# Last attention of a two-layer Perceiver kernel: tiles 2 and 3 each go alone from the turn of y to the gate's logits, with the residual added in PSUM

## The reference, cut to what matters

```python
# L1_attn: causal, 16 heads, on the layer-normed x; then a post norm
q, k, v = split(h @ Wqkv.T + bqkv)          # h = layernorm(x)
out = h + softmax(causal(q k^T / 4)) v @ Wout.T + bout
x = x + layer_norm(out) * gamma + beta
# L1_ffn: top-1 mixture of 8 experts on the layer-normed x
logits = layernorm(x) @ Wg + bg
x = x + expert_mlp(argmax(logits))          # 256 -> 1024 -> 256, fp32, GELU
```

## Time and profile before

| | |
|---|---|
| time, median of 3 runs | 528.6 us (528.46 to 528.76) |
| the profiled execution's own time | 528.27 us |
| its span, first to last instruction | 526.4 us |
| PE busy | 501.4 us (95%), 6412 matmul instructions |
| PE weight loads | 355.0 us (67%) |
| DVE busy | 324.5 us (62%) |
| ACT busy | 299.7 us (57%) |
| POOL busy | 124.3 us (24%) |
| DMA | 64.37 MB, mean 122 GB/s |

### The profile page before, as it was taken

The page is one execution under the profiler, slowest core; times in us unless marked ns, Lnnn a source line. Parts: engine busy times, 40 slices in busy tenths (PEclk is TensorE's granted clock), DMA queues, the critical chain, the costliest instruction groups (busy, mean ns, idle before and its releaser), DMA issues.

```text
span 526.4 us, 15176 instructions
## 1 busy us (share of the span) xinstructions
PE 501.4 (95%) x6412; PEld 355.0 (67%) x6426; DVE 324.5 (62%) x672; ACT 299.7 (57%) x512; POOL 124.3 (24%) x218
## 2 busy tenths in 40 slices
PE   7999998899999999789999999999999989999996
PEld 4666676556666665455767767677567658999995
DVE  4652874666666666779899889999358674101101
ACT  2465485866656653477788877887734522233311
POOL 6124126733333333430000000000042033000005
PEclk9999999999999999999999999999999999999999
DMA  8977620135555552900000000000072002998813
GB/s 311 392 269 271 236 78 2 61 76 160 147 159 149 147 158 56 384 11 2 2 4 2 4 2 4 2 4 3 2 259 66 2 0 87 263 367 278 308 60 100
DMA packets 35346, 64.37 MB, mean 122 GB/s; under 512 B 3312, under 2 KB 25328, under 8 KB 34896
## 3 DMA queue, kind: packets, MB, share of 16 engines
q1 hardware_dynamic: 34752, 62.35, 35.9%
q0 software_dynamic: 384, 1.05, 0.6%
q10 hardware_dynamic: 144, 0.01, 0.0%
HBM read 59.40 MB, written 4.00 MB: 120 GB/s over the span
## 4 chain that ended last, share of the span: by engine, by line
PE 81%; DVE 7%; POOL 3%; ACT 3%; issue 2%; DMA 2%; SPq 0%; POOLq 0%; DVEq 0%; ACTq 0%
PE ps L1352 14%; PE ps L1626 10%; PE ps L1758 9%; PE ps L1726 9%; PE ps L1772 7%; PE ps L1640 7%; PE ps L1948 7%; PE ps L1471 2%; PE ps L1484 2%; PE ps L1458 2%; PE ps L1327 2%; PE ps L1435 1%; DVE region L1128 1%; DMA attn_weights<-in_wall 1%; PE ps L1377 1%
## 5 line engine op out<-in xcount | busy, mean ns | idle before, releaser
L1128 DVE TENSOR_REDUCE region<-ps 128x1 f32<-128x512 f32 x192 | 124.2, 687 | 16.2 <-PE ps L1726 16.1
L816 ACT ACTIVATE region<-ps 128x1024 f32<-128x1024 f32 (+1 forms) x112 | 106.0, 963 | 20.9 <-PE ps L1758 20.4
L1726 PE MATMUL ps<-ctx_kT,region 96*32 96x512 bf16 x768 | 82.0, 383 | 1.7 <-DVE region L1128 0.8
L1758 PE MATMUL ps<-region,ctx_kT 98*32 98x512 bf16 x832 | 72.5, 381 | 0.6 <-ACT region L794 0.4
L1772 PE MATMUL ps<-region,ctx_v 128*32 128x128 f32 (+1 forms) x1664 | 70.2, 272 | 0.0
L1626 PE MATMUL ps<-region 128*128 128x512 f16 x264 | 62.9, 379 | 1.0 <-ACT ctx_kT L589 0.7
L1772 PEld LDWEIGHTS ps<-region,ctx_v 128*32 128x32 f32 (+1 forms) x1664 | 56.7, 109 | 9.3 <-issue 0.3
L866 ACT ACTIVATE region<-ps,ctx_v 128x128 f32<-128x128 f32 x88 | 25.2, 368 | 59.7 <-PE ps L1352 59.7
L507 POOL TENSOR_TENSOR region<-region 128x512 f32<-128x512 f32 x33 | 38.2, 1156 | 64.2 <-ACT region L741 62.8
L1640 PE MATMUL ps<-region 128*128 128x256 bf16 x384 | 47.2, 273 | 0.9 <-DVE region L1075 0.9
L1640 PEld LDWEIGHTS ps<-region 128*128 128x128 bf16 x384 | 37.4, 98 | 12.4 <-DVE region L1075 1.7
(11 more groups left out here) (234 smaller groups left out, 821.5 us busy)
## 6 DMA issues: line engine op xcount, KB each, us to landing
region<-in_w SPq DMA_DIRECT2D x15, 1024.0 KB, 8.4
region<-in_ctxT SPq DMA_DIRECT2D x8, 1601.0 KB, 8.5
region<-gates SPq DMA_DIRECT2D x30, 256.0 KB, 3.4
ctx_kT<-in_w SPq DMA_DIRECT2D x7, 1024.0 KB, 7.3
region<-in_moe SPq DMA_DIRECT2D x33, 192.0 KB, 2.4
attn_weights<-in_wall SPq DMA_DIRECT2D x1, 2152.0 KB, 22.8
slots_x<-zeros SPq DMA_DIRECT2D x1, 1408.0 KB, 10.7
attn_weights<-in_wall SPq DMA_DIRECT2D x4, 256.0 KB, 5.8
```

Of the source, the lines that this page charges most:

```text
L816: act.activation(probs[u % NP_][:, 0:512 * n_keys], ps[:, pr:pr + n_keys, :].rearrange("p b n -> p (b n)"), ACT.Exp).then_inc(mq["exp"], 1)
L1128: ins = dve.tensor_reduce(mp[g % 2][:, j // 3, j % 3:j % 3 + 1], bank(4 + n % 2), AX.X, ALU.max)
L1726: ins = pe.matmul(ps[32 * i:32 * i + 32, at, :], QT[0:KQ, b, h + i // 2, 32 * (i % 2):32 * (i % 2) + 32], kT[0:KQ, b, 512 * c:512 * c + 51 ...
L1758: ins = pe.matmul(ps[32 * c:32 * c + 32, 2 * (u % 2) + i, :], kT[0:KQ2, b, k * P + 32 * c:k * P + 32 * c + 32], QT[0:KQ2, b, 8 * r:8 * r + ...
```

## The change

- Tiles 2 and 3 each go alone through the turn of y (`tile_y`, two transposes), ACT's biased copy (`tile_y_out`), the projection, the norms, the turn of `xn` (`tile_turn`), its copy (`tile_turned`) and the logits (`tile_logits`).
- The residual `xb` of tiles 2 and 3 is no longer added by DVE: `tile_bias` multiplies it by the identity matrix into the PSUM tile as the first matmul of the projection's accumulation, and the two matmuls of the projection add to it. `tile_stats` and `tile_centre` read that PSUM tile.
- On DVE `post_add(0)` goes before unit_y(22), `norm_stats("m1", 0)` before unit_y(23), `norm_scale("m1", 0)` behind tile 2's first statistics and centre.
- Some units' steps swap places on PE, ACT and DVE.
- `keep_clock` is called with other numbers: after the turn of unit 23 and up to the last logits 2, 2, 6, 2, 6, 1, 2 and 1.
- Several steps use other PSUM banks; the three late weight loads share one semaphore; POOL waits for the last two scalings on `mq["ln"]`.

The diff, cut (the bank lists, the merged semaphore's other waits and the unchanged bodies that only move are left out):

```diff
-        tail = sems("tail", "o var rstd")
+        tail = sems("tail", "y yt o var rstd")
+        def tile_ps(t):
+            return bank(3 if t == 2 else 0, D)
...
-            sp.dma_start(wkv_l[:], a["wkvl"]).then_inc(lat_in, 16)
-            sp.dma_start(wall[:, :, 4 * D:W_TOTAL], wall_d[:, :, 4 * D:W_TOTAL]).then_inc(wall_late_in, 16)
-            sp.dma_start(gate_w[:], a["gate"].rearrange("(c p) n -> p c n", p=P)).then_inc(gate_in, 16)
+            sp.dma_start(wkv_l[:], a["wkvl"]).then_inc(late_in, 16)
+            sp.dma_start(wall[:, :, 4 * D:W_TOTAL], wall_d[:, :, 4 * D:W_TOTAL]).then_inc(late_in, 16)
+            sp.dma_start(gate_w[:], a["gate"].rearrange("(c p) n -> p c n", p=P)).then_inc(late_in, 16)
...
-            for h in range(2):
-                pool.wait_ge(half[h]["ln"], SCALED["m1"])
+            pool.wait_ge(half[0]["ln"], SCALED["m1"])
+            pool.wait_ge(mq["ln"], TT + 2)
...
+            def tile_y_out(t):
+                act.wait_ge(tail["y"], t - 1)
+                for c in range(C):
+                    o = BC["1a_v"] + c
+                    ins = act.activation(yT[:, c, t * P:(t + 1) * P], ps[:, 2 if t == 2 else 6, c * P:(c + 1) * P], ACT.Identity, bias=bcol[:, o:o + 1])
+                ins.then_inc(tail["yt"], 1)
+            def tile_turned(t):
+                act.wait_ge(mq["xt_ps"], 1 + C + t - 1)
+                act.activation(xnT[:, :, t * P:(t + 1) * P], ps[:, 4 + t, 0:256].rearrange("p (c q) -> p c q", c=C), ACT.Copy).then_inc(mq["xt"], 1)
...
+            unit_turned(16)
             unit_exp(17)
-            unit_turned(16)
...
+            unit_turned(18)
             q_out("1a", 1)
-            unit_turned(18)
...
-            y_turned("1a", 1)
+            tile_y_out(2)
+            tile_y_out(3)
             norm_turned("m1", 0)
-            norm_turned("m1", 1)
+            tile_turned(2)
+            tile_turned(3)
...
             unit_max(18)
+            unit_subtract(18)
             unit_max(19)
-            unit_subtract(18)
...
             unit_max(20)
+            unit_subtract(20)
             unit_y(18)
             unit_max(21)
-            unit_subtract(20)
...
             post_centre(0)
+            post_add(0)
             unit_y(22)
+            norm_stats("m1", 0)
             unit_y(23)
-            post_add(0)
-            norm_stats("m1", 0)
+            tile_stats(tile_ps(2), 2, 1)
+            tile_centre(2)
             norm_scale("m1", 0)
-            def tile_out(t):
-                dve.wait_ge(half[1]["bias"], BIASED["1a"])
-                dve.wait_ge(tail["o"], t - 1)
-                lk(dve.tensor_tensor(un[:, t, :], bank(3 if t == 2 else 6, D), xb[:, t, :], ALU.add))
...
-            tile_out(2)
-            tile_stats(un, 2, 1)
-            tile_centre(2)
-            tile_out(3)
-            tile_stats(un, 3, 2)
             tile_add(2, 1)
-            tile_stats(x, 2, 3)
+            tile_stats(tile_ps(3), 3, 2)
             tile_centre(3)
+            tile_stats(x[:, 2, :], 2, 3)
             tile_add(3, 2)
-            tile_stats(x, 3, 4)
+            tile_stats(x[:, 3, :], 3, 4)
             tile_scale(2, 3)
-            tile_scale(3, 4).then_inc(half[1]["ln"], 1)
+            tile_scale(3, 4)
...
+            def tile_y(t):
+                if t == 2:
+                    head_done("Q", "1a", 1)
+                pe.wait_ge(at["y"], UNITS["1a"] + 2 * t + 2)
+                for c in range(C):
+                    ins = pe.transpose(ps[:, 2 if t == 2 else 6, c * P:(c + 1) * P], y_sm[:, t, c * P:(c + 1) * P], ident)
+                ins.then_inc(tail["y"], 1)
+            def tile_bias(t):
+                head_done(*(("V", "1a", 1) if t == 2 else ("Y", "1a", 0)))
+                pe.wait_ge(half[1]["bias"], BIASED["1a"])
+                pe.matmul(tile_ps(t), ident, xb[:, t, :], start=True, stop=False, skip_group_check=True)
+            def tile_project(t):
+                pe.wait_ge(tail["yt"], t - 1)
+                for c in range(C):
+                    ins = pe.matmul(tile_ps(t), yT[:, c, t * P:(t + 1) * P], weights("1a", "o")(c), start=False, stop=(c == C - 1), skip_group_check=True)
+                ins.then_inc(tail["o"], 1)
+            def tile_turn(t):
+                pe.wait_ge(mq["ln"], TT + t - 1)
+                for c in range(C):
+                    ins = pe.transpose(ps[:, 4 + t, c * P:(c + 1) * P], xn[:, t, c * P:(c + 1) * P], ident)
+                ins.then_inc(mq["xt_ps"], 1)
+            def tile_logits(t):
+                pe.wait_ge(mq["xt"], 1 + C + t - 1)
+                ins = mm2(ps[:, 5, (t - 2) * 8:(t - 1) * 8], lambda c: xnT[:, c, t * P:(t + 1) * P], lambda c: wg(c))
+                if t == TT - 1:
+                    ins.then_inc(m1["log_ps"], 1)
...
             k_project("1a", 1)
+            unit_turn(18)
             q_project("1a", 1)
-            unit_turn(18)
+            unit_turn(19)
             unit_values(17)
             pair_scores(20)
             unit_values(18)
-            unit_turn(19)
             v_project("1a", 1)
             unit_values(19)
+            unit_turn(20)
             pair_scores(22)
-            unit_turn(20)
             y_turn("1a", 0)
+            unit_values(20)
             unit_turn(21)
-            unit_values(20)
             o_project("1a", 0)
             unit_turn(22)
             unit_values(21)
+            tile_bias(3)
             unit_turn(23)
+            tile_bias(2)
+            tile_y(2)
             keep_clock(2, 4)
             unit_values(22)
+            tile_project(2)
             keep_clock(2, 4)
             unit_values(23)
-            keep_clock(3, 4)
-            y_turn("1a", 1)
-            keep_clock(3, 7)
-            take_head("O", "1a", 1)
-            head_done("Y", "1a", 1)
-            for t in (2, 3):
-                mm2(bank(3 if t == 2 else 6, D), lambda c: yT[:, c, t * P:(t + 1) * P], lambda c: weights("1a", "o")(c)).then_inc(tail["o"], 1)
+            tile_y(3)
+            tile_project(3)
+            keep_clock(6, 1)
+            norm_turn("m1", 0)
+            keep_clock(2, 1)
+            logits(0)
+            keep_clock(6, 1)
+            tile_turn(2)
+            keep_clock(1, 1)
+            tile_logits(2)
+            keep_clock(2, 1)
+            tile_turn(3)
+            keep_clock(1, 1)
+            tile_logits(3)
...
-            norm_turn("m1", 0)
-            keep_clock(2, 7)
-            logits(0)
-            keep_clock(20, 7)
-            norm_turn("m1", 1)
-            keep_clock(2, 7)
-            logits(1)
-            keep_clock(2, 7)
+            keep_clock(2, 1)
             pe.wait_ge(m1["mask"], 1)
```

More of the change, by code:

```diff
@@ L232, in build @@
         wall_qo_in = sem("wall_qo_in")
-        wall_late_in = sem("wall_late_in")
+        late_in = sem("late_in")
         wkv_in = sem("wkv_in")
@@ L255, in build @@
         HEADS = {
[L256 to L259 removed]
+            0: "X1a0 X1a1 Y1a0".split(),
+            1: "V0x0 K1a0 K1a1 O1a0".split(),
+            2: "K0x0 X0x1 Q0x1 Y0x0 X0a0 L0a0 K0a0 V0a0 K0a1 Y0a0 Y0a1 O0a1 Q1a0 Q1a1 Xm10".split(),
+            3: "X0x0 Q0x0 K0x1 V0x1 O0x0 Y0x1 O0x1 Q0a0 X0a1 L0a1 Q0a1 V0a1 O0a0 Xm00 Xm01 V1a0 V1a1".split(),
         }
@@ L1163, in _, with tile_stats, tile_centre, tile_add @@
                     outputs(u // HS - 1)
+            def tile_stats(src, t, k):
+                if k < TT - 1:
+                    dve.wait_ge(tail["o"], k)
+                lk(dve.bn_stats(stats[:, t, :], src))
+                dve.bn_aggr(mv[:, t, :], stats[:, t, :]).then_inc(tail["var"], 1)
+                dve.wait_ge(tail["var"], k)
+            def tile_centre(t):
+                lk(dve.scalar_tensor_tensor(out=un[:, t, :], in0=tile_ps(t), scalar=mv[:, t, 0:1],
+                                            in1=brow[:, BR["gamma"]:BR["gamma"] + D], op0=ALU.subtract, op1=ALU.mult))
+            def tile_add(t, k):
+                dve.wait_ge(tail["rstd"], k)
+                dve.wait_ge(half[1]["beta"], 1)
+                lk(dve.scalar_tensor_tensor(out=x[:, t, :], in0=un[:, t, :], scalar=rstd[:, t, :],
+                                            in1=x_beta[:, t, :], op0=ALU.mult, op1=ALU.add))
+            def tile_scale(t, k):
+                dve.wait_ge(tail["rstd"], k)
+                dve.tensor_scalar(xn[:, t, :], x[:, t, :], mv[:, t, 0:1], rstd[:, t, :], ALU.subtract, ALU.mult).then_inc(mq["ln"], 1)
             add_out(0)
@@ L1607, in _ @@
             kv_project(7)
-            pe.wait_ge(gate_in, 16)
+            pe.wait_ge(late_in, 3 * 16)
             keys_turn(4, 1)
@@ L1832, in _, with logits @@
             values(NH * HS - 1)
+            wg = w("g", 0, E1)
+            def logits(h):
+                head_done("X", "m1", h)
+                for t in range(2):
+                    ins = mm2(ps[:, 4, t * 8:(t + 1) * 8], lambda c: xnT[:, c, t * P:(t + 1) * P], lambda c: wg(c))
+                ins.then_inc(m1["log_ps"], 1)
[24 more added lines that the diff above has]
```

(21 more changed lines are left out.)

27 lines of the change are left out of this document (3 added, 24 removed).

## The result

The median is 527.15 us (525.97 to 528.13, 14 runs) against 528.6 us (528.07 to 529.48, 14 runs): ratio 0.9971, interval 0.9964 to 0.9978, so 1.45 us faster, by 1.0 to 1.9. The prediction was 526.5 us, 2.1 us faster. A second measurement on another chip gave a ratio of 0.997 (0.9956 to 0.9984). The profiled execution took 527.31 us with a span of 525.2 us.

What follows compares the result with a forecast made beforehand. The prediction took the line of steps up to the last routing's start as the bound, with PE's stage following unchanged. Starting it 2.1 us earlier took the profiled 528.27 to 526.2, and the median to 526.5 us, range 524.9 to 528.3.

Steps and rivals of the forecast that it cites:

- Part 1: Order of the units ahead of half 0's first projection: 0.3 us of gain, bounds 0 and 0.5.
- Part 2: DVE queue before tile 3: moving half 0's steps ahead ends unit 23 at 420.47, costing 0.88 us on tile 3's way.
- Part 3: Tiles 2 and 3 going alone, residual off DVE: the last routing starts at 430.80 instead of 432.88, 2.1 us earlier.
- Part 4: One semaphore for three loads, other PSUM banks and POOL's wait on another counter: no effect.
- 1.9 around: Time of the profiled execution outside its 526.4 us span, within 528.27 us; 2.1 us was taken off the whole.
- (a): Rival: fillers cost nothing, DVE and POOL set the end; routing 3.7 us earlier, 524.9 us; chance 0.10.
- (b): Rival: no measurable change, small shapes cost 1.8 us or parts 1 and 2 disappoint; 527.6 to 528.6 us; chance 0.17.
- (c): Rival: with fewer fillers PE's clock falls to its lower level ahead of the dispatch; +7.5 us, 533.7 us; chance 0.06.

Runs made afterwards that it cites:

- e1: The changed kernel without its 18 fillers between tile 3's projection and the last logits; 527.57 us, ratio 0.9973.
- e3: The kernel before with only the swaps of the units' steps on PE, ACT and DVE; 528.3 us, ratio 0.999.
- e8: The changed kernel with DVE's add and m1 statistics of half 0 put back behind unit 23's values; 528.06 us, ratio 0.998.
- e11: The changed kernel with 12 of those 18 fillers, placed where PE waits, and without the two between tile 2's projection and unit 23's values; 525.71 us, ratio 0.9938.
- e2: The changed kernel with twelve fillers in each of the two places where it has six; 530.01 us, ratio 1.0028.
- e4: The kernel before with only the three late weight loads put on one semaphore; 528.83 us, ratio 1.0001.
- e9: The changed kernel, unchanged, timed again on another chip; 527.21 us, ratio 0.997.
- e5: The changed kernel with the residual of tiles 2 and 3 added again by DVE instead of by the identity matmul; 527.83 us, ratio 0.9979.
- e7: The changed kernel with turn, copy and logits of tiles 2 and 3 done together again, behind the same fillers; 526.44 us, ratio 0.9957.
- e12: e11 with five fillers added in the waits around tile 3's y turn, two before it and three after; 525.27 us, ratio 0.9936.

## Why the prediction was right

**What bounds the kernel.** The start of the last routing decides: from there to the dispatch 3.97 us (3.96), from there to the end 89.63 (89.54), as said. In the traces of all variants but e1 the first is 3.96 or 3.97, and the second 89.5 to 89.6.

**Part 1** was taken at 0.3 us with bounds of 0 and 0.5. It is 0.53 at half 0's projection and 0.55 at the routing in e3, just above the upper bound. From half 0's y turn to the projection pass 1.67 us in e3 (1.65 forecast, 2.09 before). The term that was mis-sized is the 0.15 us put against it for DVE: the y turn doesn't start 0.15 later but 0.11 earlier (13.28 us after the norm turn instead of 13.39). By the diff unit 21's subtraction stands behind unit 18's values in both kernels; what moved is unit 20's, to an earlier place.

**Part 2** had the right number and the wrong carrier. Less the 0.80, POOL's root ended at 417.27 (417.53 in the schedule, 0.26 better, mostly by part 1), unit 22 at 418.81 (418.99), unit 23 at 420.54 (420.47). That unit 23's end agrees within 0.07 is luck: the root's lead was lost because unit 23's values came late on PE (0.26 us in the row of its reciprocal), not because DVE was held. e8 shows it (unit 23 no earlier with DVE free) and e11 (0.40 earlier with two fillers gone). The schedule had followed DVE's queue and not PE's own: tile 2's y turn and its projection (0.97 us of PE, 418.61 to 419.58) moved in ahead of unit 23's values, where two groups of two fillers stood already.

**Part 3** came out to 0.1 us at each step, less the 0.80: tile 3's projection 421.75 (421.81), half 0's turn 424.01 (424.00), its logits 425.30 (425.31), DVE's last scaling 427.47 (427.5), tile 3's turn 429.26 (429.29), its logits 430.11 (430.17), the last routing 430.76 (430.80). The terms: two transposes 0.38 to 0.44 (0.40 taken), two biased copies 0.63 (0.62), copy of 128x256 0.38 to 0.39 (0.40), logits 0.61 (0.60), statistics from PSUM 0.42 to 0.43 (no difference from SBUF, as taken), centre from PSUM 0.48, twelve more fillers 2.59 in e2 (0.216 each). The Trainium skill (ScalarE: Activation LUTs, What ACT_TABLE_LOAD costs) gives 186 ns and 0.833 ns a column for an activation without a bias pointer, by which the copy would have been an estimated 0.40 us; the trace's 0.38 agrees, and the bounds of 0.31 and 0.60 could have been narrower.

**Part 4**: nothing, by e4.

**The sum.** 2.1 us was forecast and the traces show 2.12, but the first measurement of the medians shows 1.45, and 527.15 instead of 526.5. One term of the sum was mis-sized: "1.9 around" the span was carried over to the changed kernel. The time outside the span is 1.89 us on average in 103 executions of the kernel before (1.84 to 1.94) and 2.17 in the 14 of the changed kernel (2.11 to 2.21; 2.15 in e9). That is some 0.27 us more, outside what the traces cover. e3 and e4 have the old value (1.90, 1.91), e5 has 2.07 and every other variant 2.15 to 2.20, so neither the swaps nor the semaphore bring it; what does stays open. Part of the rest is the clock: four of the 26 executions of the changed kernel ran below a mean of 0.999, three of them, in e9, with a median of 529.25. On e9's chip the executions at full clock differ by 529.0 - 526.84 = 2.2 us, and their spans by 2.4. In the first measurement 13 of 14 were at full clock and their median, 527.09, is still only 1.5 below 528.6, in spans an estimated 1.8 (1.5 + 0.27). Scatter upstream, which is as large as 1.2 us between executions of one kernel, can hide the remaining 0.3 in one measurement; that it does so here was not shown.

**The rivals.** (a) *Fillers cost nothing* is false: twelve more cost 2.59, six fewer give 1.20, and the path through DVE and POOL alone isn't reached even in e1, where PE waits 1.59 us for DVE and the way is 32.87. (b) *Small shapes cost their bounds*: none did. (c) *The clock falls* did not come true in the changed kernel's first profile, with 1.00 throughout, but the mechanism is real: in e1 in all executions, in the changed kernel in some. It was priced as one fall in front of the dispatch at +7.5 us. (533.7 adds this to the profiled execution's 528.27; from the median, as in the forecast, it would be 534.0.) The falls seen cost less. e1's lasts about as long, from 428 to 436 us, but nearly all of it comes ahead of PE's own stage, where waits and fillers take up part of it: 0.45 us ahead of the routing and 1.3 from there to the dispatch. e9's is short, 423 to 427 us; summed over the rows above, the missing clock is 0.44 + 0.50 + 0.50 + 0.27 = 1.7 us, which is what the way lost. A chance for a small, occasional fall, with a price of 1 to 2 us, was missing among the cases.

**What the prediction didn't ask.** By its own schedule both tiles are scaled at 427.5 and tile 2 is turned at 427.5. It didn't see that taking them alone then only adds hand-overs: e7's pair is 0.86 us shorter there, half of it by two fillers off the path. And it put 2.59 us of fillers on the path without asking how many of them the clock needs.

## What to carry to other kernels

Fillers are instructions like any other: where the engine is late against its suppliers, each costs its full time, and where it waits it costs nothing, so put them into the rows that carry a wait in brackets (five in e12 cost 0.0 us) and take them from the stretches without one, but not all of them (e1). Splitting a step into tiles costs hand-overs where both tiles are there already (some 0.4 us in after, by e7). It should pay where the second tile comes clearly later than PE could take the first. In e11 the last scaling ends at 428.42 and the first turn starts at 427.61; a pair turned 0.15 us behind the scaling, with e7's 2.39 us to the routing, would put it at an estimated 430.96 instead of 430.53. No run tried that. When a step moves between queues, write down the order of both engines: the carrier of unit 23 was in the queue that the schedule took for free.

## What was not expected of the hardware

- The same instructions of the same kernel ran at a granted clock of 1.00 in one execution and at 0.50 for some 3 us in another; of the kernel before, 17 of 103 executions had a mean clock below 0.999, of the changed kernel 4 of 26. The Trainium skill (TensorE: Matmul & The Clock Gate, Part 1) says that the monitor's window runs on its own and doesn't start with the kernel; that would explain it, and no run here can show it.
- The start of the last attention scatters by 1.2 us between traces of one unchanged kernel (397.10 and 398.28), with two more DMA pieces (3.16 and 3.61 us) in the chain of the later one.
- The changed kernel spends some 0.27 us more outside its span than the kernel before (2.16 against 1.89 us on average of 26 and 103 executions). The cause is open.
- Statistics and centring read PSUM as fast as SBUF (0.42 to 0.43 and 0.48 us for 128x256).
